# Half of the attention probabilities of eight tiles turned by DMAs instead of TensorE, with heads paired 16 apart and the first FFN's halves in tile order

## What is computed

```
x = LN(x + attention(x))      # 32 heads of 16, 8 key/value heads, RoPE, causal softmax
x = LN(x + ffn0(x))           # 4-bit weights (GPTQ), 512 -> 1376 -> 512, gate * sigmoid(gate) * up
x = LN(x + hydra(x))          # 512 -> 128, gelu, two passes of a scan over a batch of 4, 128 -> 512
x = LN(x + ffn1(x))           # 4-bit weights, 512 -> 1792 -> 512, silu(gate) * up
```

## Time and profile before

| | before |
|---|---|
| median of three runs | 1486.59 us |
| the profiled execution's own time | 1488.29 us |
| its span in the trace | 1486.5 us |
| TensorE (PE) busy | 1420.9 us, 96% |
| VectorE (DVE) busy | 1076.0 us, 72% |
| ScalarE (ACT) busy | 787.8 us, 53% |
| POOL busy | 677.0 us, 46% |
| DMA, mean | 76 GB/s |

### The profile page before, as it was taken

One profiled execution on the slowest core, in us unless ns is written; L12 is line 12 of the kernel. 1 busy time (PEld: TensorE's weight loads), 2 busy tenths in 40 slices (PEclk: granted clock), 3 DMA queues, 4 the chain that ended last, 5 costly groups with the idle time before them and its releaser, 6 DMA issues.

```text
span 1486.5 us, 33018 instructions
## 1 busy us (share of the span) xinstructions
PE 1420.9 (96%) x12054; PEld 1050.4 (71%) x12054; DVE 1076.0 (72%) x2371; ACT 787.8 (53%) x1731; POOL 677.0 (46%) x867
## 2 busy tenths in 40 slices
PE   7889999999999999999999899999999999999998
PEld 4446876786777688688678477586857777676875
DVE  6877778778776767788787869695878768686121
ACT  4776777777677667677676333334333342331211
POOL 5555756756667575442101344442425352541211
PEclk8669999999999999999999999999999999999999
DMA  8744535644655453311210100450001000100000
GB/s 248 187 99 100 132 101 144 128 101 105 136 117 120 124 133 86 107 42 30 65 57 13 64 1 10 170 205 29 15 1 40 12 9 1 43 15 9 8 15 15
DMA packets 154499, 112.80 MB, mean 76 GB/s; under 512 B 73882, under 2 KB 137602, under 8 KB 153442
## 3 DMA queue, kind: packets, MB, share of 16 engines
q1 hardware_dynamic: 153100, 110.62, 28.1%
q10 hardware_dynamic: 1238, 0.07, 0.1%
HBM read 75.00 MB, written 19.92 MB: 64 GB/s over the span
## 4 chain that ended last, share of the span: by engine, by line
PE 74%; DVE 13%; issue 4%; DMA 3%; POOL 3%; ACT 3%; SPq 1%; DVEq 0%; POOLq 0%; ACTq 0%
PE ps L1645 14%; PE ps L1817 13%; PE ps L1717 8%; PE ps L1837 8%; PE ps L1660 5%; PE ps L1707 4%; PE ps L1605 4%; PE ps L1632 4%; PE ps L1730 3%; PE ps L1579 2%; PE ps L1767 2%; DVE xraw L1419 2%; PE ps L1608 2%; PE ps L1710 2%; PE ps L1754 1%
## 5 line engine op out<-in xcount | busy, mean ns | idle before, releaser
L1817 PE MATMUL ps<-x3h,w1gu 128*128 128x256 f16 x1792 | 298.8, 273 | 6.1 <-DVE prod L1489 3.8
L1114 ACT ACTIVATE pth<-ps 128x512 f16<-128x512 f32 (+1 forms) x352 | 196.5, 559 | 147.3 <-PE ps L1717 143.1
L1249 DVE TENSOR_REDUCE nmax<-ps 128x1 f32<-128x384 f32 (+3 forms) x352 | 221.0, 636 | 70.1 <-PE ps L1710 67.4
L1120 ACT ACTIVATE Pe<-ps,nmax 128x256 f32<-128x256 f32 (+3 forms) x512 | 246.8, 531 | 17.2 <-DVE nmax L1249 16.9
L1817 PE MATMUL ps<-x3l,w1gu 128*128 128x256 f16 x896 | 244.8, 273 | 0.0
L1244 DVE TENSOR_TENSOR ptl<-ps,pth 128x512 f16<-128x512 f32 (+1 forms) x352 | 219.1, 633 | 23.6 <-ACT pth L1114 21.5
L1717 PE MATMUL ps<-identf,Pe 128*128 128x128 f32 x1280 | 206.1, 281 | 1.4 <-DVE ptl L1244 1.4
L1817 PEld LDWEIGHTS ps<-x3h,w1gu 128*128 128x128 f16 x1792 | 175.9, 98 | 30.0 <-DVE prod L1489 5.9
L1024 POOL TENSOR_TENSOR int1l<-prod,int1h 128x256 f16<-128x256 f32 x112 | 97.0, 875 | 161.1 <-ACT int1h L1206 160.9
L1717 PEld LDWEIGHTS ps<-identf,Pe 128*128 128x128 f32 x1280 | 143.5, 145 | 29.5 <-issue 7.9
L1707 PE MATMUL ps<-kT,qT 128*128 128x256 f16 (+3 forms) x512 | 140.6, 309 | 10.9 <-ACT Pe L1120 10.2
(11 more groups left out here) (246 smaller groups left out, 3335.4 us busy)
## 6 DMA issues: line engine op xcount, KB each, us to landing
w1gu<-w_gu SPq DMA_DIRECT2D x7, 1024.0 KB, 8.9
x_dram<-xr SPq DMA_DIRECT2D x18, 256.0 KB, 2.3
xr<-in_x SPq DMA_DIRECT2D x16, 256.0 KB, 4.4
x2a<-x_dram SPq DMA_DIRECT2D x4, 1024.0 KB, 5.5
vq<-in_q1g SPq DMA_DIRECT2D x28, 128.0 KB, 2.3
vz<-in_z1g SPq DMA_DIRECT2D x28, 128.0 KB, 3.0
vs<-in_s1g SPq DMA_DIRECT2D x28, 128.0 KB, 3.3
w_gu<-vh SPq DMA_DIRECT2D x56, 64.0 KB, 1.9
```

The source lines that it names most:

```text
L1114: act.activation(pth[:, u % 3, 0:g * w], ps[:, 2 + u % 2, 0:g * w], ACT.Copy).then_inc(sem("pth"), 1)
L1120: ins = act.activation(Pe[:, u % 2, x * w:(x + 1) * w], ps[:, u % 2, x * w:(x + 1) * w], ACT.Exp, bias=nmax[:, u % 4, x:x + 1])
L1249: dve.tensor_reduce(nmax[:, u % 4, 0:g], ps[:, u % 2, 0:g * w].rearrange("p (g w) -> p g w", g=g), AX, ALU.max, negate=True).then_inc(sem( ...
L1817: ins = pe.matmul(ps[:, bank, piece * H2:piece * H2 + H2], w1gu[:, j // 2, 2 * piece + pw, k, cols], px[:, k, h * H2:h * H2 + H2], start=( ...
```

## The change

1. **Turning by DMA.** In tiles 3, 6, 7, 11, 12, 13, 14 and 15, the units whose first head has h % 4 in (0, 2) skip TensorE's transposes: every unit of tile 11, which holds two heads a unit, and every second unit of the others. That is 8 x 16 = 128 of the 352 units. ScalarE copies `Pe` to float16 in a new buffer `stp` of three slots (`p_hi`), VectorE or, in tiles 12 to 15, POOL makes the low half next to it (`p_lo`), and one DMA transpose on the SP queue turns both, up to 1024 columns, into `pt`, which replaces `pth` and `ptl` with six slots. The exponential of unit u + 2 waits for `p_lo` of u where it waited for `ptr`. `pv` waits for the DMA.
2. **Heads 16 apart.** The query projection reads its weights in another order, so that partition pairs of `qT` hold heads h and h + 16; the key/value groups 0 to 3 then live in one half of the partitions only and 4 to 7 in the other, and `kT` has 8 blocks a tile where it had 16. `group_of_head` names the group, and `attn` is written back in the old order. `st_hi` and `k_lo` keep their number of instructions, each half as long; tile 0's staging has three steps where it had four.
3. **Halves in tile order.** `LATE` is empty: the halves are (0,1), (2,3), ... (14,15), with no store to DRAM and no load. `FFN0_AT` has new ranks. Half (10,11), which hydra's stage 0 needs, is now the sixth of eight where it was the fifth.
4. The semaphores of the first FFN's loads and of the second's weight loads are shared (`ld_w`).

```diff
+def group_of_head(h):
+    return NKV // 2 * (h % 2) + h // 2 // NREP
+NPT, NST = 6, 3
+PT_TILES, PT_HEADS = (3, 6, 7, 11, 12, 13, 14, 15), (0, 2)
+LO_POOL = (12, 13, 14, 15)
-LATE = (6, 7)
+LATE = ()
+PT_DMA = [u for u in range(NUNIT) if UNITS[u][0] in PT_TILES and UNITS[u][3] % 4 in PT_HEADS]
+PT_PE = [u for u in range(NUNIT) if u not in PT_DMA]
+def low_made(engine, sem, u):
+    engine.wait_ge(sem("p_lo_pool" if UNITS[u][0] in LO_POOL else "p_lo_dve"), LO_NO[u] + 1)
+def pt_turned(engine, sem, u):
+    engine.wait_ge(sem(f"ld_pt{PT_NO[u] % NST}"), 16 * (PT_NO[u] // NST + 1))
...
-        A("ACT", "exp", u, 200 * g + 0.75 * c, [("nmax", u), ("ptr", u - 2) if u >= 2 else None], u - 1)
+        A("ACT", "exp", u, 200 * g + 0.75 * c, [("nmax", u), ("p_lo" if u - 2 in PT_DMA else "ptr", u - 2) if u >= 2 else None], u - 1)
+        if u in PT_DMA:
+            A("ACT", "p_hi", u, 170 + 0.8 * c, [("exp", u), ("pt", PT_DMA[m - NST]) if m >= NST else None], u)
+            if t in LO_POOL:
+                A("POOL", "p_lo", u, 200 + 2.5 * c, [("p_hi", u)], u)
+            else:
+                A("DVE", "p_lo", u, 150 + 1.07 * c, [("p_hi", u)], u)
+            ready = A("SP", "pt", u, 4000, [("p_lo", u), ("pv", u - NPT) if u >= NPT else None], u)
...
-FFN0_AT = [(32, 100), (107, 150), (150, 215), (193, 266), (266, 339), (407, 412), (412, 427), (404, 432)]
+FFN0_AT = [(25, 153), (107, 161), (157, 191), (280, 340), (336, 568), (606, 680), (680, 750), (743, 887)]
...
-        kT = lb("kT", [P, NKV * 2, KSLOT * P], F16)
+        kT = lb("kT", [P, NKV, KSLOT * P], F16)
-        pth = lb("pth", [P, 3, 512], F16)
-        ptl = lb("ptl", [P, 3, 512], F16)
+        pt = lb("pt", [P, NPT, 1024], F16)
+        stp = lb("stp", [P, NST, 1024], F16)
...
+        def probabilities_lo(engine, name, u):
+            engine.wait_ge(sem("p_hi"), PT_NO[u] + 1)
+            engine.tensor_tensor(stp[:, n, c:2 * c], Pe[:, u % 2, 0:c], stp[:, n, 0:c], ALU.subtract).then_inc(sem(f"p_lo_{name}"), 1)
+        def sp_turn(sp, u):
+            low_made(sp, sem, u)
+            if u >= NPT:
+                sp.wait_ge(sem("pv"), u - NPT + 1)
+            sp.dma_start_transpose(out=pt[:, at, 0:2 * c].rearrange("p (a n) -> p a n", n=P), in_=stp[:, PT_NO[u] % NST, 0:2 * c]).then_inc(sem(f"ld_pt{PT_NO[u] % NST}"), 16)
...
+            if kind == "p_hi":
+                act.wait_ge(sem("exp"), u + 1)
+                if n >= NST:
+                    pt_turned(act, sem, PT_DMA[n - NST])
+                act.activation(stp[:, n % NST, 0:g * w], Pe[:, u % 2, 0:g * w], ACT.Copy).then_inc(sem("p_hi"), 1)
...
-                pe.matmul(ps[:, bank, :], xT[:, k, :], wqkv[:, k, 0:512], start=(k == 0), stop=(k == KD - 1))
+                pe.matmul(ps[:, bank, :], xT[:, k, :], wqkv[:, k, 0:512].rearrange("p (v h c) -> p h v c", v=2, c=HD), start=(k == 0), stop=(k == KD - 1))
...
-                              kT[:, 2 * (h // NREP) + h % 2, first:first + w], start=True, stop=False)
+                              kT[:, group_of_head(h), first:first + w], start=True, stop=False)
```

More of the change, by code:

```diff
@@ L174, with w1_landed @@
 NC1 = len(CH1)
+PT_DMA = [u for u in range(NUNIT) if UNITS[u][0] in PT_TILES and UNITS[u][3] % 4 in PT_HEADS]
+PT_PE = [u for u in range(NUNIT) if u not in PT_DMA]
+PT_NO = {u: n for part in (PT_DMA, PT_PE) for n, u in enumerate(part)}
+LO_NO = {u: n for x in (True, False) for n, u in enumerate(u for u in PT_DMA if (UNITS[u][0] in LO_POOL) == x)}
+def low_made(engine, sem, u):
+    engine.wait_ge(sem("p_lo_pool" if UNITS[u][0] in LO_POOL else "p_lo_dve"), LO_NO[u] + 1)
+def pt_turned(engine, sem, u):
+    engine.wait_ge(sem(f"ld_pt{PT_NO[u] % NST}"), 16 * (PT_NO[u] // NST + 1))
+def w1_landed(n):
+    return 32 * len(range(n, NC0, NPK)) + 16 if n < NPK else 16
 NLD1A, NLD1B = 12, 4
@@ L285, in way_in @@
         A("POOL", "qk", t, 2000, [("qk_s", t)], r)
-        A("ACT", "st_hi", t, 1950, [("qk", t)] + (staged(t - 1) if t else []), r)
+        A("ACT", "st_hi", t, 1750, [("qk", t)] + (staged(t - 1) if t else []), r)
+        A("POOL", "k_lo", t, 800, [("st_hi", t)], r, chain="q_lo")
         A("POOL", "q_lo", t, 2200, [("st_hi", t)], r)
-        A("POOL", "k_lo", t, 1500, [("st_hi", t)], r, chain="q_lo")
         if t not in PE_STAGED:
-            for kind, lo, free in (("dq", "q_lo", q_after(t)), ("dk", "k_lo", k_after(t))):
+            for kind, lo, free in (("dk", "k_lo", k_after(t)), ("dq", "q_lo", q_after(t))):
                 A("SP", kind, t, 4500, [(lo, t), ("score", free - 1) if free else None], r)
@@ L906, in sp_stream @@
                     else:
[L907 removed]
+                        sp.dma_start(w1gu[:, key, :, :, :], w1gu_dram[key]).then_inc(sem(f"ld_w{key}"), 16)
                 if kind == "store":
@@ L995, in pool_stream @@
                     pool_job(pool, kind, key)
+                if kind == "p_lo":
+                    probabilities_lo(pool, "pool", key)
                 if kind == "w0_lo":
@@ L1068, in act_job @@
                 act.activation(stq[:, :, 0:4:2, :], bcast(q, 2, 2), ACT.Copy)
-                act.activation(stk[:, :, 0, 0, 0:2, :], bcast(k, 2, 2), ACT.Copy)
-                act.activation(stk[:, :, 1, 1, 0:2, :], bcast(k, 2, 2), ACT.Copy).then_inc(sem("st_hi"), 1)
+                for part, kv in enumerate(KV_PARTS):
+                    ins = act.activation(stk[:, kv, part, 0:2, :], bcast(k[:, kv, :], 2, 2), ACT.Copy)
+                ins.then_inc(sem("st_hi"), 1)
             if kind in ("etq0", "etk0"):
                 b, i = TILE[key]
-                act.wait_ge(sem("str"), 4 * key + (1 if kind == "etq0" else 3))
+                act.wait_ge(sem("str"), 3 * key + (1 if kind == "etq0" else 3))
                 src = ps[:, JOB_BANK[kind[1:], key], :].bitcast(F16).rearrange("p (a n) -> p a n", a=8)
@@ L1513, in dve_stream @@
                     dve_attention(dve, own, kind, key)
+                if kind == "p_lo":
+                    probabilities_lo(dve, "dve", key)
                 if kind == "deq":
@@ L1555, in bank_free @@
                     pe.wait_ge(sem("ste_act"), 2 * key + (1 if kind == "tq0" else 2))
-                if kind in ("tq1", "tk1"):
-                    pe.wait_ge(sem("ste_dve"), 2 * key + (1 if kind == "tq1" else 2))
+                if kind == "tq1":
+                    pe.wait_ge(sem("ste_dve"), key + 1)
                 if kind == "atr":
@@ L1726, in pe_attention @@
                     dst = ps[:, 4, (h % OG) * 64:(h % OG) * 64 + VW]
-                    for part, src in ((0, pth), (1, ptl)):
+                    for part in (0, 1):
                         for p in range(i + 1):
-                            c = x * w + p * P
-                            ins = pe.matmul(dst, src[:, u % 3, c:c + P], V[:, b % 2, token_tile(b, i, p), h // NREP, :],
+                            c = (part * g + x) * w + p * P
+                            ins = pe.matmul(dst, pt[:, u % NPT, c:c + P], V[:, b % 2, token_tile(b, i, p), group_of_head(h), :],
                                             start=(part == 0 and p == 0), stop=(part == 1 and p == i))
```

113 lines of the change are left out of this document (63 added, 50 removed).

## The result

The changed kernel takes **1508.48 us** (1507.69 to 1512.74) against 1487.26 for the kernel before beside it: a ratio of **1.0148, interval 1.0135 to 1.0161**. The forecast was 1454, in a range to 1482. TensorE does less, as planned, and the time goes up by 21 us.

The account below looks back on a forecast made before the run. TensorE was taken to set the pace, with hydra's serial passes a parallel limit after 815. Hydra's start 814.6 - 51 + 18 + 5 = 787, plus 150 for stage 0 and 517 to the end, gave 1454 us, range 1430 to 1482.

Parts of the forecast that it names:

- 0 to 15 us, and I take 5 us more: Attention: late DMA transposes delay TensorE by 0 to 15 us, taken as 5, since FFN 0's pieces fill most gaps.
- the prediction's own signs of being wrong: Included hydra's start outside 775 to 800 us and TensorE's waits for the DMAs exceeding 15 us.
- The upper bound of 4.8 us: Landing time of a DMA transpose, from the median of earlier ones with twice as many columns.
- six slots cover it: Product with V: six slots, ten us, cover a turn's low half, issue and landing (1.2 + 4.8), if SP is free.
- the 51 us: Attention: 464 of 1280 transposes leave TensorE at 0.11 us each, 51 us less.
- The 18: FFN 0 in tile order: 18 us of TensorE work move from behind hydra's start to ahead of it.
- Part 2's strided read: Query projection: reading its weights with a stride was taken to cost TensorE nothing.
- the room I gave the first pass: Hydra's stage 0: with less FFN work, the first pass can fall from 67 us to the second's 58.
- TensorE is all that counts: Hydra's passes shorten or the fill is shifted, so all 51 us count: 1435 us, chance 0.20.
- The sixth half is late: Before hydra: TensorE does FFN 0's sixth half after the attention, hydra starts 20 us later: 1474 us, chance 0.17.
- The exponential waits for POOL: Tiles 12 to 15: the exponential's shared buffer slot waits for POOL's low half; 1508 us at a 4.3 us cycle, chance 0.06.
- VectorE and POOL block each other: Tiles 3, 6, 7 and 11: low halves reading SBUF twice collide with POOL, 43 us if all does: 1497, chance 0.08.

Follow-up runs that it names:

- plan6: The changed kernel with a DMA turn planned at 6.0 us where it was 4.0: 1505.5 us, ratio 1.0129 to the kernel before.
- heads_only: The changed kernel with no unit turned by DMA and the old late halves and ranks, heads still 16 apart: 1494.6 us, ratio 1.0056 to the kernel before.
- light_loads: The changed kernel with the second FFN's loads of zeros and scales cut to 16 columns after two chunks (wrong weights): 1483.6 us.
- tiny_turns: The changed kernel with each DMA turning only 128 columns, as many turns, wrong results: 1484.1 us, ratio 0.9966 to the kernel before.
- tuned_last4_tile_order: The changed kernel with turns in tiles 12 to 15 alone, halves in tile order and searched ranks: 1484.2 us, ratio 0.9979 to the kernel before.
- tuned_last4: The changed kernel with turns in tiles 12 to 15 alone, planned at 5.0 us, late halves and searched ranks: 1466.4 us.
- tuned_none: The changed kernel with no turns, heads 16 apart, late halves and searched ranks: 1471.5 us, ratio 0.9896 to the kernel before.
- first4_old_order: The changed kernel with turns in tiles 3, 6, 7 and 11 alone and the old late halves and ranks: 1518.2 us.
- last4_old_order: The changed kernel with turns in tiles 12 to 15 alone and the old late halves and ranks: 1501.8 us.
- last4: The changed kernel with turns in tiles 12 to 15 alone, keeping its halves in tile order and its new ranks: 1491.7 us.

## Why the prediction was wrong

**The step that failed** is the one that priced the turns' waits: "0 to 15 us, and I take 5 us more". TensorE idled 38 us more up to hydra's start. 19 of them go with the cut loads and 20 with turns of 128 columns (76.0 us idle, then 56.6 and 56.0), so about half is the bytes of turns and loads beside one another. The other half stays: the turns' fixed part and the order share it, and no run splits it. Two of the prediction's own signs of being wrong came, hydra's start outside 775 to 800 and waits for the DMAs over 15 us. The landing time was taken from the earlier trace rows, from transposes that came 15 times in a run, at a DMA share of 0.50. 128 more transfers change that share. It rose to 0.73 with stretches of 50 us at 0.83, the landing had a tail to 7.7, and the loads of the weights became late in return: POOL waited 48.5 us for scales (20.5, 18.5 and 9.5 by kind), for 22 before. The upper bound of 4.8 us held for the median and not for the tail. From the end of ScalarE's copy to the landing a turn of the first four tiles took 6.8 us at the median and 10.7 at most, where I had counted 6.0. The argument "six slots cover it" fell with it: plan6 shows that the attention is held even where V's products don't wait.

**What held.** The transposes' 0.11 us, the 51 us, and the form of the sum: with 38 in the place of 5 and 25 in the place of 18 it gives 827 for hydra's start, 4 us short of the measured one. The 18 was too small because it left both last halves whole behind the start, 528 gate and up matmuls, and 444 stood there. Part 2's strided read cost nothing on TensorE, but the order that came with part 2 cost 7 us in heads_only. From hydra's start to FFN 1's start I had 150 us for 154 before. It took 157. The first pass took 66 us to the end of its output product for 65 before, the second 63 for 60. **Less work for TensorE didn't shorten the passes**: from the last product with V to the stage's first low half (`x3l`) it is 153 us before, 156 with light_loads, tiny_turns and the change, 154 in tuned_last4_tile_order, 155 in tuned_last4, 153 in tuned_none, and from there to the end 519 to 520 in the kernel before, the change and tuned_last4. So the room I gave the first pass, down to 58, wasn't there, and the span of these kernels is the end of the last product with V plus 672 to 676 us. The three runs with the old ranks on the changed steps stand apart (heads_only 163, first4_old_order 166, last4_old_order 160), which is how an order that fits badly costs there.

**The rivals.** *TensorE is all that counts*: refuted, as TensorE idles 33 us in stage 0. *The sixth half is late*: hydra's input was on its way at 789.4, 41 us ahead of the start. *The exponential waits for POOL*: it waited 5.5 us in all, and POOL's low halves took 1.16 and 0.91 us, as priced. This rival forecast 1508 and the kernel took 1508.5, which is luck, since its wait wasn't there. *VectorE and POOL block each other*: seen, and small. These are VectorE's low halves from two SBUF inputs and from PSUM, in the changed kernel:

```profile
L1321 DVE TENSOR_TENSOR pt<-ps,pt 128x512 f16<-128x512 f32 x144 | 97.3, 681 | 17.7 <-ACT pt L1182 17.1 <-DVE A L1431 0.3
...
L796 DVE TENSOR_TENSOR stp<-Pe,stp 128x512 f16<-128x512 f32 x48 | 40.5, 845 | 5.6 <-ACT stp L1188 5.5
...
L796 DVE TENSOR_TENSOR stp<-Pe,stp 128x384 f16<-128x384 f32 x16 | 10.5, 655 | 2.0 <-ACT stp L1188 2.0
```

With 384 columns the form from PSUM takes 548 ns, so 48 x 0.164 + 16 x 0.107 = 10 us on VectorE. tiny_turns keeps them (826 and 675 ns) and is 24 us faster, so they aren't the loss that went with the bytes. I had all mechanisms of the slower side on engines, and the one that decided was on the transfers.

Why turning in tiles 12 to 15 loses 7 us with the old ranks and gains 5 with searched ones, the traces show in part. Ahead of the last product with V, last4_old_order does 59 of FFN 0's down matmuls more than heads_only, 13 us, idles 55 us for 40, and has a mean granted clock of 0.97 for 1.00 in the last 246 us, 7 us by estimate. -25 + 13 + 15 + 7 = 10, and its last product comes 11 us later. With searched ranks next to nothing of FFN 0 moved, the idle time grew by 11 us (45 for 35) and the clock was 0.99 for 1.00. Why the planner moved the matmuls at equal ranks, no run took apart.

## What to carry to other kernels

Price a new transfer in the stretch where it will run, with the transfers that run there already, and ask what it delays as well as what delays it: a median landing from a quiet place is no upper bound. Look for a serial stage behind the edit whose length doesn't react to less work on the busiest engine; then only what reaches its start counts. And where a planner lays the queues, compare edits each at its own best order, since the order alone was worth 23 us here and the turning 5. And look at the granted clock too: where TensorE waited more, it was lower in two of the runs.

## What the runs showed of the hardware that was not expected

- A DMA transpose of 1024 float16 columns in SBUF occupies SP for 1.23 us and lands in 2.7 us at least, 3.1 at the median after most of the weights' loads (last4), 3.9 in the changed kernel, 4.5 in its first four tiles. With 128 columns it still takes SP 1.10 us and lands in 2.2 at least: most of it is fixed. It also fills the DMA engines: 64 turns raised their share from 0.20 (heads_only, 571 to 809 us) to 0.55 (last4_old_order, 574 to 820), which is (246 x 0.55 - 238 x 0.20) / 64 = 1.4 us of all 16 engines a turn, by estimate.
- At the end of stage 0 the granted clock fell to 0.66 from 960 to 992 us. Two float32 matmuls of the "in" product took 2.05 us there for 0.93 before, which is the lower of the two levels (1.2 and 2.4 GHz). Ahead of it TensorE had been busy for 52 of 62 us (from 898), and in the kernel before for 55 of 58 (from 881) with no such fall.
- The same subtraction takes VectorE 845 ns on average from two SBUF inputs beside a busy POOL, and 681 from PSUM and SBUF. With no POOL operation beside it the form from two SBUF inputs took 679 to 694 for these 512 columns, and with some beside it up to 1867. The Trainium skill, SBUF — State Buffer, section Who interferes with whom, says that only the form with two SBUF inputs contends with POOL's reads; the trace agrees.
